# Gram matmuls whose moving side has 224 columns in place of 256

## The chip, the cores and the metric

The kernel runs on one core of a Trainium2 chip. Its metric is the device time of one execution in microseconds (us); lower is better. Before the change it took 532.54 us in the median of 3 runs (530.84 to 533.41).

## The reference, cut to what matters

A batch of 2048 samples, each with 27 feature vectors of 128 numbers. For each sample the dot products of every two features are formed (the gram matrix, 27 x 27), its 351 entries under the diagonal are put behind the sample's 128 dense numbers, and four layers with relu and one output row follow:

```python
dots = jnp.einsum('bfd,bgd->bfg', bottom_output, bottom_output)      # 2048 x 27 x 27
pairs = dots[:, _TRIL_I, _TRIL_J]                                    # 351 per sample
x = jnp.concatenate([bottom_mlp_output, pairs, pad], axis=1)         # 480
for w, b in ((w0, b0), (w1, b1), (w2, b2), (w3, b3)):                # 1024, 1024, 512, 256
    x = jax.nn.relu(x @ w.T + b)
return x @ w_out.T + b_out
```

Everything is float32.

## The kernel before, in words

Each engine has a program of its own, written out by hand; semaphores order them. The batch goes in 8 chunks of 256 samples. While TensorE multiplies the layers of chunk c, the grams of chunk c+1 are made between these products, and the first few of c+2. `chunk_steps` writes the order: after every 18 products of a chunk (6 in the first chunk) one list of `unit_steps` is put in, for one unit of 16 samples. A chunk has 16 units. A unit is four groups of four samples; a group is one matmul.

To reach nearly float32 results with the faster float32r matmuls, each operand is split into a high part that float32r holds exactly and the low remainder. A layer's product is then three matmuls (`products`, L726): high weights by high data, high weights by low data, low weights by high data, each with 128 x 128 weights and 256 columns moving.

A unit goes through these steps:

- SyncE loads its rows (L458). VectorE turns them, 32 x 32 at a time (L921), into `raw`, with the 128 numbers on the partitions and 32 columns for each sample, 27 of them features and 5 more.
- ScalarE writes the high part into `xt` (L805), VectorE the low part (L926), 27 columns of each sample's 32. `xt` holds for each group first 128 high columns, then 128 low ones. The 5 columns left of each sample are zero from a memset.
- TensorE multiplies (`gram`, L688): the 128 high columns are the weights, and the 256 columns, high and low, move. That gives high by high and high by low for all four samples against each other; only each sample against itself is of use. Two groups fill one PSUM bank of 512 numbers, and a unit has two banks. A gram waits until ScalarE has read the unit two before (`parts_done`).
- ScalarE reads the used blocks out of PSUM (`gram_parts`, L817), one instruction for each of the four samples' places: 27 partitions by 2 x 4 x 27 numbers, by the view `gram_found`.
- GpSimd adds high by low to high by high (L564), VectorE turns the high by low part (L945), GpSimd adds that too into `grams` (L571).

When a chunk's 16 units are done, SyncE writes `grams` to HBM (L405, `blocks<-grams`), reads them back in another order into `pairs` (L410), and then loads rows for the chunk after. The layers' results go from PSUM through ScalarE (`drain`, L833), then VectorE makes the high part (L952) and GpSimd the low (L579); TensorE's next layer waits for these.

The grams of chunk 0, before any layer, are made in another way: TensorE transposes (L647) and plain float32 matmuls with 128 x 128 weights and 108 columns (`gram_early`, L671). The weights are transposed by L642.

Of the kernel before, what the change touches and what calls it, by code (L numbers as in the profile page):

```python
# [11 lines left out]
BATCH, FEATS, DIM = 2048, 27, 128  # L12
PAIRS = FEATS * (FEATS - 1) // 2
LAYERS = [(DIM + PAIRS + 1, 1024), (1024, 1024), (1024, 512), (512, 256)]
P = 128
# [5 lines left out]
GROUP = 4  # L21
RUN = CHUNK // GROUP
GROUP_ROWS = GROUP * FEATS
QUAD = 32
# [27 lines left out]
ACC_RING, TURN_RING, GRAM_RING = 2, 2, 2  # L52
GRAM_BANKS = 2

XT_RING, XT_LAG = 4, 2
# [5 lines left out]
GATHER_AFTER, FIRST_UNIT, LATE_HOOK = 6, 11, 38  # L61
AHEAD, AHEAD_HOOK = 5, 49
FULL_ROWS = 112
EARLY_SLOTS = 8
RAW_RING = 2
EARLY_XT = 2 * XT_RING
# [157 lines left out]
def dlrm_program(nc, x, x_mlp, w0, b0, w1, b1, w2, b2, w3, b3, w_out, b_out, y):  # L224
    weights = [w0, w1, w2, w3]
    biases = [b0, b1, b2, b3]
    with ExitStack() as ctx:
        def sb(name, shape, dt=F32):
            return ctx.enter_context(nc.sbuf_tensor(name, shape, dt))
# [4 lines left out]
        def shared(*specs):  # L234

            with ExitStack() as inner:
                return [inner.enter_context(nc.sbuf_tensor(n, s, F32)) for n, s in specs]
# [13 lines left out]

        early_rows, = shared(("early_rows", [P, EARLY_SLOTS, UNIT_GROUPS, DIM]))
        h_b = sb("h_b", [P, 8, 2, CHUNK], F32R)
# [5 lines left out]
        xt = sb("xt", [P, XT_RING, UNIT_GROUPS, 2, GROUP * QUAD], F32R)  # L259
# [13 lines left out]
        gram_ps = ctx.enter_context(nc.psum_tensor("gram_ps", [P, GRAM_RING * GRAM_BANKS, 512], F32))  # L273
# [48 lines left out]
        step_n, step_u, step_c = FEATS * DIM, UNIT_GROUPS * GROUP * FEATS * DIM, CHUNK * FEATS * DIM  # L322
        full_dims = [[DIM, FULL_ROWS], [GROUP * step_n, UNIT_GROUPS], [1, DIM]]
        x_full = bass.AP(x.tensor, 0, [[step_c, CHUNKS - 1], [step_u, UNITS]] + full_dims)
# [68 lines left out]
        def quad_of(s):  # L393

            return slice(QUAD * s, QUAD * s + FEATS)

        def gram_found(u, s):

            b = u % GRAM_RING * GRAM_BANKS
            return gram_ps[quad_of(s), b:b + GRAM_BANKS, :].rearrange("p a (b h n) -> p h (a b) n", h=2, n=P)[  # L400
                :, :, :, QUAD * s:QUAD * s + FEATS]

        def spill_quad(engine, s):

# [7 lines left out]
        def early_rows_of(u):  # L412

            if u < EARLY_SLOTS:
                return early_rows[:, u]
            u -= EARLY_SLOTS
            return rows[:, u] if u < ROWS_RING else early_rows[:, u - ROWS_RING]
# [17 lines left out]
        def _(sp):  # L435
            def load_early(u):
                if u >= EARLY_SLOTS + ROWS_RING:

                    sp.wait_ge(turned, u - EARLY_SLOTS - ROWS_RING + 1)
                sp.dma_start(early_rows_of(u)[0:FULL_ROWS], x_full[0, u]).then_inc(early_loaded[u], 16)  # L440

            def load_rows(d, u):
                if isinstance(d, int) and d == 1 and u < ROWS_RING:

                    sp.wait_ge(turned, EARLY_SLOTS + u + 1)
                else:
# [152 lines left out]
        def _(pe):  # L599
# [75 lines left out]
            def gram(d, u):  # L675

                pe.wait_ge(xt_done, d * UNITS + u + 1)
                if isinstance(d, int) and d == 1 and u < GRAM_RING:
                    if u == 0:

                        pe.wait_ge(w_done, LATE_WEIGHTS)
                        pe.wait_ge(xt_zeroed, 2)
                else:

                    pe.wait_ge(parts_done, (d - 1) * UNITS + u + 1 - GRAM_RING)
                for j in range(UNIT_GROUPS):
                    at = j % 2 * 2 * P
                    last = nc.tensor.matmul(gram_ps[:, u % GRAM_RING * GRAM_BANKS + j // 2, at:at + 2 * P], xt[:, u % XT_RING, j, 0],  # L688
                                            xt[:, u % XT_RING, j].rearrange("p h n -> p (h n)"), start=True, stop=True)
                last.then_inc(gram_done, 1)  # L690

            def turn_mlp(d):
# [49 lines left out]
            def chunk(c):  # L742
                for step in steps_of(c):
                    if step[0] == "mm":
                        products(c, *step[1:])
                    elif step[0] == "gram":
                        gram(c + step[1], step[2])
                    elif step[0] == "weights":
                        turn_weights(step[1])
                    elif step[0] == "out" and not (isinstance(c, int) and c == 0):  # L750
                        out_row(c - 1)
                    elif step[0] == "mlp":
                        turn_mlp(c + 1)
# [20 lines left out]
        def _(act):  # L774
# [32 lines left out]
            def gram_parts(d, u):  # L807

                act.wait_ge(gram_done, d * UNITS + u + 1)
                if isinstance(d, int) and d == 1 and u < 2:  # L810

                    act.wait_ge(parts_zeroed, 1)
                else:

                    act.wait_ge(grams_done, d * UNITS + u - 1)
                for s in range(GROUP):
                    last = nc.scalar.activation(parts[quad_of(s), u % 2, :, :, 0:FEATS], gram_found(u, s), ACT.Copy)  # L817
                last.then_inc(parts_done, 1)
# [232 lines left out]
```

## Time and profile before

| | |
|---|---|
| median of 3 runs | 532.54 us |
| the profiled execution | 532.41 us |
| its span, first to last instruction | 530.6 us |
| TensorE matmuls busy | 501.3 us (94%) |
| VectorE, ScalarE, GpSimd busy | 289.1, 333.7, 260.6 us |
| gram matmuls, L688 | 448, 72.9 us of busy time |

The busy time of matmuls counts from the start of one to its modelled end, and these overlap: a matmul of 283 ns is followed by the next start 120 ns later. What a matmul costs in a dense stretch is therefore read as the distance of starts, not as its duration. The timeline merges neighbours; the distance is got from the starts of two rows and the count between them.

### The profile page before, as it was taken

Reading aid. Unit: us, or ns where it says so; the run is one execution under the profiler, and the core shown is the slowest. Engines: PE = TensorE matmul, PEld = TensorE weight load, DVE = VectorE, ACT = ScalarE, POOL = GpSimd, SP = SyncE. Lnnn points to the kernel's source line nnn. Section 1 sums busy time; section 2 is a strip of 40 time slices with the busy share of each in tenths; the row PEclk is TensorE's granted clock in tenths of the full one; section 3 lists DMA queues with packets and bytes.
Section 4 is the critical chain, followed back from the end, with each engine's and each line's share of the span. In section 5 each row is a group of like instructions: output and inputs, shape, how many; then the busy total and the mean of one; then the engine's idle time right before and its main releaser. Section 6 shows DMA issues by size and latency. Waiting matters only on the chain.

```text
span 530.6 us, 13442 instructions
## 1 busy us (share of the span) xinstructions
PE 501.3 (94%) x4073; PEld 491.5 (93%) x4073; DVE 289.1 (54%) x646; ACT 333.7 (63%) x844; POOL 260.6 (49%) x467
## 2 busy tenths in 40 slices
PE   6968987799999999999999999999999999999996
PEld 6858987699999899999999999999999999999996
DVE  3764877466753576446762676356753676232101
ACT  4644799747974588737883698657873698433112
POOL 2800356424865267634864287625764387524221
PEclk9996999999999999999999999999999999999999
DMA  8997677644563566356663656266653662210000
GB/s 246 264 312 156 196 119 114 114 77 81 89 109 75 94 105 104 55 109 113 102 96 67 116 96 106 44 125 109 99 79 79 117 103 43 49 47 1 1 1 0
DMA packets 281054, 53.23 MB, mean 100 GB/s; under 512 B 265126, under 2 KB 279230, under 8 KB 281022
## 3 DMA queue, kind: packets, MB, share of 16 engines
q1 hardware_dynamic: 279090, 52.22, 51.9%
q10 hardware_dynamic: 1932, 0.61, 0.5%
q8 instruction: 17, 0.28, 0.2%
q14 instruction: 15, 0.12, 0.1%
HBM read 45.71 MB, written 7.09 MB: 99 GB/s over the span
## 4 chain that ended last, share of the span: by engine, by line
PE 66%; DMA 11%; SPq 7%; ACT 5%; POOL 4%; issue 4%; DVE 3%; POOLq 0%; DVEq 0%; ACTq 0%
PE acc L726 52%; PE gram_ps L688 8%; DMA blocks<-grams 5%; ACT parts L817 3%; SPq L410 3%; DMA early_rows<-in_r_bottom_output_dram 2%; SPq L405 2%; PE gram_ps L642 2%; DMA rows<-in_r_bottom_output_dram 2%; PE gram_ps L671 2%; POOL grams L571 1%; SPq L458 1%; POOL h_a L579 1%; POOL parts L564 1%; DMA pairs<-blocks 1%
## 5 line engine op out<-in xcount | busy, mean ns | idle before, releaser
L726 PE MATMUL acc<-h_a,w_hi 128*128 128x256 f32 x1152 | 214.4, 285 | 3.9 <-POOL h_a L579 2.6
L726 PEld LDWEIGHTS acc<-h_a,w_hi 128*128 128x128 f32 x1152 | 179.1, 192 | 6.6 <-POOL h_a L579 4.3
L817 ACT ACTIVATE parts<-gram_ps 27x216 f32<-27x216 f32 x448 | 152.9, 341 | 25.7 <-PE gram_ps L688 18.5
L833 ACT ACTIVATE h_full<-acc,small_t 128x256 f32<-128x256 f32 x172 | 81.5, 474 | 132.2 <-PE acc L726 128.7
L726 PE MATMUL acc<-h_a,w_lo 128*128 128x256 f32 x576 | 162.8, 283 | 0.0
L579 POOL TENSOR_TENSOR h_a<-h_full,h_a 128x256 fp32r<-128x256 f32 x96 | 72.2, 752 | 139.6 <-DVE h_a L952 139.6
L726 PEld LDWEIGHTS acc<-h_a,w_lo 128*128 128x128 f32 x576 | 110.3, 192 | 0.0
L726 PE MATMUL acc<-h_b,w_hi 128*128 128x256 f32 x512 | 93.9, 284 | 0.0
L726 PE MATMUL acc<-x,w_hi 128*128 128x256 f32 x480 | 90.7, 288 | 0.0
L579 POOL TENSOR_TENSOR h_b<-h_full,h_b 128x256 fp32r<-128x256 f32 x64 | 47.4, 740 | 83.1 <-DVE h_b L952 83.1
L564 POOL TENSOR_TENSOR parts<-parts 128x128 f32<-128x128 f32 x112 | 82.4, 736 | 6.1 <-ACT parts L817 5.5
L926 DVE TENSOR_TENSOR xt<-raw,xt 128x432 fp32r<-128x432 f32 x112 | 82.0, 732 | 4.2 <-ACT xt L805 4.2
L921 DVE STREAM_TRANSPOSE raw<-rows 128x512 f32<-128x512 f32 x112 | 78.4, 700 | 6.2 <-DMA rows<-in_r_bottom_output_dram 6.0
L726 PEld LDWEIGHTS acc<-h_b,w_hi 128*128 128x128 f32 x512 | 79.7, 192 | 0.0
L688 PE MATMUL gram_ps<-xt 128*128 128x256 f32 x448 | 72.9, 285 | 6.3 <-ACT parts L817 5.9
L726 PEld LDWEIGHTS acc<-x,w_hi 128*128 128x128 f32 x480 | 75.5, 194 | 1.4 <-issue 0.8
L952 DVE CAST h_a<-h_full 128x256 fp32r<-128x256 f32 x96 | 32.2, 336 | 80.1 <-ACT h_full L833 80.1
L726 PE MATMUL acc<-h_b,w_lo 128*128 128x256 f32 x256 | 72.4, 283 | 0.0
L688 PEld LDWEIGHTS gram_ps<-xt 128*128 128x128 f32 x448 | 61.6, 192 | 8.8 <-DVE xt L926 4.4
L952 DVE CAST h_b<-h_full 128x256 fp32r<-128x256 f32 x64 | 18.8, 294 | 93.2 <-ACT h_full L833 93.2
L726 PE MATMUL acc<-x,w_lo 128*128 128x256 f32 x240 | 68.3, 285 | 0.0
L805 ACT ACTIVATE xt<-raw 128x432 fp32r<-128x432 f32 x112 | 62.5, 558 | 1.8 <-DVE raw L921 1.4
(59 smaller groups left out, 439.5 us busy)
## 6 DMA issues: line engine op xcount, KB each, us to landing
rows<-in_r_bottom_output_dram SPq DMA_DIRECT2D x444, 64.0 KB, 2.1
blocks<-grams SPq DMA_DIRECT2D x30, 216.0 KB, 3.9
w_raw<-in_L_rec_w_dram SPq DMA_DIRECT2D x6, 1024.0 KB, 7.9
early_rows<-in_r_bottom_output_dram SPq DMA_DIRECT2D x12, 224.0 KB, 5.7
stage_pairs<-in_L_rec_w_dram SPq DMA_DIRECT2D x1, 1408.0 KB, 9.2
w_raw<-in_L_rec_w_dram SPq DMA_DIRECT2D x2, 512.0 KB, 8.5
mlp_rows<-r_bottom_mlp_output_dram SPq DMA_DIRECT2D x8, 128.0 KB, 2.2
pairs<-blocks SPq DMA_DIRECT2D x8, 126.0 KB
```

The costliest lines, as they stand in the source:

```text
L405: engine.dma_start(blocks[:, :, s * RUN:(s + 1) * RUN], grams[QUAD * s:QUAD * (s + 1)]).then_inc(spilled, 16)
L410: engine.dma_start(pairs[q % P:q % P + nf * nk, q // P], src).then_inc(gathered[q // P], 16)
L564: nc.gpsimd.tensor_tensor(hh, hh, hl, ALU.add).then_inc(sum_done, 1)
L579: nc.gpsimd.tensor_tensor(h[:, m, 1, :], h_full[:, slot % 2, :], h[:, m, 0, :].bitcast(F32), ALU.subtract).then_inc(split_done, 1)
L688: last = nc.tensor.matmul(gram_ps[:, u % GRAM_RING * GRAM_BANKS + j // 2, at:at + 2 * P], xt[:, u % XT_RING, j, 0], xt[:, u % XT_RING, j]. ...
L726: last = nc.tensor.matmul(acc_slot(c, slot), weight(wp, layer, m, k), in_tile(layer, k, xp), start=(k == 0 and n == 0), stop=(k == K_TILES ...
L805: nc.scalar.activation(xt_part(u, 0), raw_cols(u), ACT.Copy).then_inc(xt_hi_done, 1)
L817: last = nc.scalar.activation(parts[quad_of(s), u % 2, :, :, 0:FEATS], gram_found(u, s), ACT.Copy)
L833: nc.scalar.activation(h_full[:, slot % 2, :], acc_slot(c, slot), ACT.Relu, bias=small_t[:, slot:slot + 1]).then_inc(drained, 1)
L921: nc.vector.transpose(raw[:, u % RAW_RING].rearrange("p j n -> p (j n)"), rows[:, r].rearrange("p j n -> p (j n)")).then_inc(raw_turned, 1)
L926: nc.vector.tensor_tensor(xt_part(u, 1), raw_cols(u), xt_part(u, 0).bitcast(F32), ALU.subtract).then_inc(xt_done, 1)
L952: nc.vector.tensor_copy(h[:, m, 0, :], h_full[:, slot % 2, :]).then_inc(high_done, 1)
```

## The change

The gram matmul's moving side reads, of each sample's 32 columns, the first 28 (27 features and one zero column) in place of all 32: 2 x 4 x 28 = 224 columns. Its outputs lie packed 28 apart, 224 numbers from the same starts in the bank. ScalarE's view of PSUM follows. The weights' side, the number of instructions, their order and all waits stay; on TensorE the 112 rows of four gram matmuls stand in the same places with 128x224 for 128x256.

```diff
+EVEN = FEATS + 1
...
         def gram_found(u, s):
 
             b = u % GRAM_RING * GRAM_BANKS
-            return gram_ps[quad_of(s), b:b + GRAM_BANKS, :].rearrange("p a (b h n) -> p h (a b) n", h=2, n=P)[
-                :, :, :, QUAD * s:QUAD * s + FEATS]
+            found = gram_ps[quad_of(s), b:b + GRAM_BANKS, :].rearrange("p a (b n) -> p (a b) n", n=2 * P)
+            return found[:, :, 0:2 * GROUP * EVEN].rearrange("p j (h n) -> p h j n", h=2)[
+                :, :, :, EVEN * s:EVEN * s + FEATS]
...
                 for j in range(UNIT_GROUPS):
                     at = j % 2 * 2 * P
-                    last = nc.tensor.matmul(gram_ps[:, u % GRAM_RING * GRAM_BANKS + j // 2, at:at + 2 * P], xt[:, u % XT_RING, j, 0],
-                                            xt[:, u % XT_RING, j].rearrange("p h n -> p (h n)"), start=True, stop=True)
+                    found = gram_ps[:, u % GRAM_RING * GRAM_BANKS + j // 2, at:at + 2 * GROUP * EVEN]
+                    both = xt[:, u % XT_RING, j].rearrange("p h (s f) -> p (h s) f", f=QUAD)[:, :, 0:EVEN]
+                    last = nc.tensor.matmul(found, xt[:, u % XT_RING, j, 0], both, start=True, stop=True)
                 last.then_inc(gram_done, 1)
```

## Rows read from the trace of the kernel before

**Rows 1.** The page, part 1: busy time of each engine.

```profile
PE 501.3 (94%) x4073; PEld 491.5 (93%) x4073; DVE 289.1 (54%) x646; ACT 333.7 (63%) x844; POOL 260.6 (49%) x467
```

**Rows 2.** Stretches: length, busy us and count of each engine, clock, DMA, GB/s.

```profile
80.00:120.00 40.00, 33.57 (x269) 31.97 (x269) 24.57 (x51) 28.49 (x71) 16.88 (x29) 1.00 0.58 101
120.00:180.00 60.00, 59.87 (x497) 59.42 (x496) 34.97 (x77) 42.21 (x111) 34.60 (x54) 1.00 0.50 86
41.00:44.00 3.00, 2.96 (x15) 2.96 (x15) 0.43 (x1) 0.56 (x2) 0.00 (x0) 0.50 0.72 135
```

**Rows 3.** Timeline of TensorE in a dense stretch: start, length, instruction, count.

```profile
128.77 0.64 PE L688 MATMUL gram_ps<-xt 128*128 128x256 f32 x4
129.25 0.40 PE L726 MATMUL acc<-x,w_hi 128*128 128x256 f32 x2
129.49 0.28 PE L726 MATMUL acc<-x,w_lo 128*128 128x256 f32 x1
```

**Rows 4.** Line L688: duration ns min/median/max, first and last start, form.

```profile
L688 PE MATMUL gram_ps<-xt x448: 278/283/357, 65.5 to 456.9; 128*128 128x256 f32 x150
```

**Rows 5.** Tile `parts` from 120 us on, same columns: readouts and GpSimd's sums.

```profile
L817 ACT ACTIVATE parts<-gram_ps x382: 320/343/348, 120.0 to 458.3; 27x216 f32<-27x216 f32 x191
L564 POOL TENSOR_TENSOR parts<-parts x96: 457/826/911, 122.3 to 458.7; 128x128 f32<-128x128 f32 x96
```

**Rows 6.** Who TensorE waited for, 65 to 120 us: total, times, longest.

```profile
PE gram_ps L688 <- ACT parts L817: 5.9, 9, 0.8
```

**Rows 7.** The same view, 120 to 500 us.

```profile
PE acc L726 <- POOL h_a L579: 2.6, 5, 1.0
PE acc L726 <- ACT h_full L833: 1.0, 5, 0.2
```

**Rows 8.** Timeline of ScalarE, 83 to 89 us.

```profile
83.82 1.41 ACT L817 ACTIVATE parts<-gram_ps 27x216 f32<-27x216 f32 x4 [0.19 <-POOL grams L571]
85.26 0.57 ACT L805 ACTIVATE xt<-raw 128x432 fp32r<-128x432 f32 x1
85.85 1.41 ACT L817 ACTIVATE parts<-gram_ps 27x216 f32<-27x216 f32 x4
87.28 0.47 ACT L833 ACTIVATE h_full<-acc,small_t 128x256 f32<-128x256 f32 x1
```

**Rows 9.** The chain that ended last, 221 to 244 us: start, length, what.

```profile
222.75 0.49 PE gram_ps L688 x4
225.29 0.59 POOL grams L571
228.23 4.43 DMA blocks<-grams
237.60 1.94 DMA rows<-in_r_bottom_output_dram
241.96 0.87 POOL h_a L579
```

**Rows 10.** Timeline, the two output-row matmuls with one column of weights.

```profile
308.17 0.39 PE L739 MATMUL turned_ps<-h_a,ones 128*1 128x256 f32 x2
308.40 0.40 PE L726 MATMUL acc<-x,w_hi 128*128 128x256 f32 x2
```

**Rows 11.** Line L671, the plain float32 grams of chunk 0.

```profile
L671 PE MATMUL gram_ps<-xt_full x128: 275/275/421, 7.0 to 28.7; 128*128 128x108 f32 x128
```

**Rows 12.** Timeline of TensorE there.

```profile
26.15 2.84 PE L671 MATMUL gram_ps<-xt_full 128*128 128x108 f32 x24
```

**Rows 13.** Timeline of weight loads: float32 grams, then float32r grams.

```profile
26.17 2.54 PEld L671 LDWEIGHTS gram_ps<-xt_full 128*128 128x128 f32 x22
...
304.93 0.55 PEld L688 LDWEIGHTS gram_ps<-xt 128*128 128x128 f32 x4
```

**Rows 14.** Timeline of TensorE at half clock: layer products, 256 columns.

```profile
42.59 0.63 PE L726 MATMUL turned_ps<-x,w_hi 128*128 128x256 f32 x2
43.02 0.41 PE L726 MATMUL turned_ps<-x,w_lo 128*128 128x256 f32 x1
```

## The prediction

> **What bounds the kernel now.** I read the busy times first. TensorE's matmuls are busy for 94% of the span, no other engine for more than 63% [rows 1]. Then the stretches, to see whether that holds everywhere: from 120 us on TensorE is busy for 59.87 of 60 us, while from 80 to 120 us it is busy for 33.57 of 40 [rows 2]. So there are two regimes. In the long one each matmul that becomes shorter makes the kernel shorter. In the short one, where the grams of chunk 1 lie between the products of chunk 0, something else sets the pace: TensorE waits nine times for ScalarE's readout of grams, 5.9 us in all [rows 6], and ScalarE's instructions stand there nearly end to end (83.82 + 1.41 = 85.23, the next at 85.26; 85.26 + 0.57 = 85.83, the next at 85.85) [rows 8].
>
> Third, the pace of matmuls in the dense stretch. Four gram matmuls start at 128.77 and the next product at 129.25: 0.48 / 4 = 120 ns each. The two products behind them take 0.24 / 2 = 120 ns each [rows 3]. The duration of one, 283 ns [rows 4], is no cost, since they overlap. The gram matmuls cost 448 x 120 ns = 54 us, and the change touches only these.
>
> Last, the chain at a chunk's end. After the last gram of a chunk (222.75) it runs through GpSimd's sum, the writing of the grams to HBM, a load of rows, and GpSimd's split of the last layer's input at 241.96, for which TensorE waits [rows 9]. From 120 us on that wait adds up to 2.6 us over five boundaries [rows 7]. The matmuls of two units lie beside this chain, not in it.
>
> **The change, part by part.** Nothing is added, removed or moved; 448 matmuls (112 units of four) [rows 4] stream 224 columns in place of 256. Three further things change in form.
>
> 1. The streaming. At the full level of the clock, 2.4 GHz (granted clock 1.00 [rows 2]), 256 columns at one a cycle would be 106.7 ns and 224 would be 93.3 ns, 13.3 ns less. That one column a cycle fits is seen at the other level: where the granted clock was 0.50, three products took (43.02 - 42.59) / 2 = 215 ns each [rows 14], which is 256 columns at 1.2 GHz (213). At the full level 120 - 107 = 13 ns are on top. The question is whether 120 falls by all of the 13.3.
>
> 2. The weight load. Each gram matmul brings a new 128 x 128 block of float32 weights, and this stays. No row shows float32r with fewer than 256 columns, so I bound it. The nearest rows are the float32 grams of chunk 0: 24 instructions with 128 x 128 weights and only 108 columns take 2.84 us, or (2.84 - 0.28) / 23 = 111 to 112 ns each [rows 12]. Their weight loads keep the same distance, (2.54 - 0.19) / 21 = 112 ns [rows 13], where I took 0.19 us for one load from (0.55 - 0.19) / 3 = 120 ns in the second row there. With so few columns it is most likely the load that sets 112 ns. The other side: with one column of weights and 256 moving, a matmul takes (308.40 - 308.17) / 2 = 115 ns [rows 10]. So streaming alone is 115, loading alone about 112, and both together 120. With 224 columns streaming alone would be 115 - 13 = 102, under the load. The ends are therefore: 120 (no gain, whatever sets 120 does not see the columns) and 120 - 13.3 = 106.7 (all of it gained). I take 112, the row with the same weights and fewer columns: 8 ns less for each matmul.
>
> The Trainium skill ("TensorE: Matmul & The Clock Gate", section "LDWEIGHTS (loading the stationary operand)") says that a load's time goes with the number of weight columns alone, P/1.2 ns, which is 107 ns for 128: by it the floor would be 107 and the gain at most 13 ns. The measured 112 decides.
>
> 3. The moving side is read in 8 runs of 28 numbers with gaps of 4, before in one run. The float32 grams read 4 runs of 27 with gaps of 5, and take 112 ns all the same [rows 12]. So I put this at nothing; if each run cost a cycle, 8 x 0.42 = 3 ns would be hidden under the load as well.
>
> 4. ScalarE reads the same 216 numbers from 27 partitions, 28 apart in place of 32. Nothing in the rows has such a step alone; the ends are 0 and a tenth of its 343 ns [rows 5] up or down, and I take 0. In the dense stretch it is hidden (42.21 of 60 us busy [rows 2]).
>
> The sum. Dense stretch: the units of chunks 2 to 7 are 96 (the GpSimd sums from 122 us on are x96 [rows 5]), so 384 matmuls x 8 ns = 3.1 us. Of these the two units beside each of five end-of-chunk chains, 40 matmuls x 8 = 0.3 us, gain nothing if that chain [rows 9] holds its length: the wait for GpSimd grows by as much. That leaves 2.8 us. Chunk 1's 16 units, 64 matmuls x 8 = 0.5 us, lie where ScalarE sets the pace [rows 6, 8]; TensorE comes 32 ns earlier to the same wait. I take 0.1 of the 0.5. The sum is 2.9 us, with 2.8 and 3.6 as ends for 8 ns.
>
> What is late next: nothing new in the dense stretch. ScalarE, at 42.21 of 60 us, gets each gram 32 ns earlier, and SyncE's writing of a chunk's grams starts earlier with it.
>
> The profiled execution took 532.41 us, so the sum gives 529.5; the median of the runs shown is 532.54, which gives 529.6. That is 0.55% faster. This measurement can tell about 0.5%, 2.7 us, from no change, so the forecast sits on that edge.
>
> **The rivals.**
>
> *Nothing is gained.* The 120 ns are set by the pair of a 128-column load and its matmul, whatever streams. For it: load and matmul both keep exactly 120 [rows 3, 13], and alone they are 112 and 115, so 120 is neither of them. Against it: at 108 columns the same load goes at 112 [rows 12]. Time: 532.5.
>
> *All of the streaming is gained.* The load is hidden and 120 falls to 107 ns. 384 x 13.3 = 5.1, plus part of chunk 1's 0.85 and less 0.5 at the boundaries: about 5 us, up to 6.0 (448 x 13.3). Time: 527.5, down to 526.5. Against it: no matmul with 128 x 128 weights is seen under 111 ns [rows 12]. The skill's rule for the distance of matmuls (the same page, "Back-to-back issue gap", N/2.4 + 2.5 ns) stands on this side, with 109 ns for 256 columns and 96 for 224; the trace's 120 for 256 already disagrees with it.
>
> *The matmul falls out of its fast form, and the kernel is slower.* Every float32r matmul here has exactly 256 columns; the trace has none with fewer. If float32r with fewer columns went as plain float32 does, each gram matmul would cost what L671's does: that line has 64 matmuls in the code (16 units of four) and 128 in the trace, two for each, 2 x 112 = 224 ns for 108 columns [rows 11, 12]. The lower end is 224 ns for our 224 columns too, (224 - 120) x 448 = 47 us, and by columns it is 224 x 224 / 108 = 465 ns, 155 us. Time: 579 to 687. It decides from 126 ns for a gram matmul, since 6 x 448 = 2.7 us. For it: only that no row excludes it, and that float32 already shows such a doubling in this trace. Against it: the loads of float32 and float32r go alike (112 and 120), which looks like one machine with a floor, not two modes.
>
> *The gapped reading costs.* Place: the same matmuls, 120 to about 128 ns, up to 3.6 us slower, 536. The float32 grams' 112 with gaps speaks against it.
>
> **How the numbers follow.** Forecast (a gram matmul at 111 to 114 ns, 1.8 to 3.6 us less): 0.50. Nothing gained: 0.24. All gained: 0.12. Out of the fast form: 0.10. Gapped reading: 0.04. The forecast lies on the edge of 0.5%, so a little over half of it counts as faster: 0.28 of 0.50, the rest as no change. Faster: 0.28 + 0.12 + 0.01 from noise = 0.41. No change: 0.22 + 0.23 = 0.45. Slower: 0.10 + 0.04 = 0.14. The range reaches from the end of "all gained" (526.5, less half a us of spread) to "nothing gained" with the spread that the three runs show (533.41) and a part of the gapped reading: 526.0 to 534.5. It leaves the third rival out. The forecast's own range is 528.3 to 531.5.
>
> **What would show it.** In the timeline of a dense stretch, four gram matmuls from the first start to the next product's start: 0.45 us by the forecast (0.48 before), 0.48 if nothing is gained, 0.43 if all is, 0.9 or more with twice the instructions if they fall out of the fast form. The distance of their weight loads should equal it. TensorE's wait for GpSimd at the five boundaries should rise by some 0.05 us each, and its waits for ScalarE in chunk 1's stretch should grow by about 0.3 us in all. The readouts of ScalarE should stay at 343 ns, the products of the layers at 120. The prediction is wrong if a gram matmul's distance is under 110 or over 115 ns, or if it is 112 and the time does not follow.

## The result and the profile after

The changed kernel took 530.85 us in the median of 22 runs (528.97 to 534.53), the kernel before 534.40 beside it (22 runs, 530.16 to 537.26). The ratio is 0.9956, interval 0.9938 to 0.9975: about 2.4 us, a small gain that is clear of noise. (The two medians alone lie 3.55 us apart, a ratio of 0.9934. I go by the ratio and its interval, which two profiles agree with.) The forecast was 529.6 from 532.54, a ratio of 0.9945. So the time and the direction of that number hold. The chances beside it did not: they had "no change" as the likeliest (0.45 to 0.41), because they treated 0.5% as the least that can be told. The interval here is 0.2% wide on either side and leaves "no change" out.

The profiled execution took 531.61 us. The page's rows that answer to [rows 1, 4]:

```profile
span 529.8 us, 13442 instructions
...
PE 497.5 (94%) x4073; PEld 486.9 (92%) x4073; DVE 289.7 (55%) x646; ACT 333.4 (63%) x844; POOL 260.6 (49%) x467
...
L692 PE MATMUL gram_ps<-xt 128*128 128x224 f32 x448 | 68.7, 276 | 6.8 <-ACT parts L820 6.3
```

There are still 448 instructions, not twice as many, so nothing fell out of the fast form. The span is only 0.8 us shorter, though. The reason stands ahead of anything the change touches. These rows give, for L688 and L692 from chunk 2 on, the first and last start, before and after:

```profile
L688 PE MATMUL gram_ps<-xt x384: 279/283/283, 118.6 to 456.9; 128*128 128x256 f32 x192
```

```profile
L692 PE MATMUL gram_ps<-xt x384: 270/274/278, 120.3 to 456.1; 128*128 128x224 f32 x192
```

Chunk 2's first gram comes 1.7 us later in the profile after, and the first gram of all (67.2 against 65.5) is as much later. Over the profiles of this study that first gram started anywhere from 62.9 to 69.0 us, while weights and rows are loaded. So profiles are compared here by what follows chunk 2's first gram: 530.6 - 118.6 = 412.0 us before, 529.8 - 120.3 = 409.5 after. I call this the rest. It is 2.5 us shorter, which agrees with the ratio; a second profile of the changed kernel gives 409.6.

The dense stretch, TensorE's timeline, answering to [rows 3]:

```profile
212.99 0.60 PE L692 MATMUL gram_ps<-xt 128*128 128x224 f32 x4
213.43 0.41 PE L729 MATMUL acc<-h_a,w_hi 128*128 128x256 f32 x2
213.67 0.28 PE L729 MATMUL acc<-h_a,w_lo 128*128 128x256 f32 x1
```

Four gram matmuls now take 213.43 - 212.99 = 0.44 us, 110 ns each, where they took 0.48. From one unit to the next it is 2600 ns in place of 2640: 10 ns for each matmul, 3.8 us over 96 units. Only 2.5 of it arrived. TensorE's waits from 120 us on, answering to [rows 7]:

```profile
PE acc L729 <- POOL h_a L581: 3.0, 5, 1.1
PE acc L729 <- ACT h_full L836: 1.0, 5, 0.2
```

At the five ends of chunks it waits 0.4 us more than before. The remaining 1.0 us does not appear in this view; the one of the weight loads (PEld) shows where it is. The first fence is of before, the second of after, both for PEld from 120 us on:

```profile
PEld acc L726 <- POOL h_a L579: 4.3, 7, 1.2
```

```profile
PEld acc L729 <- POOL h_a L581: 5.7, 12, 1.3
```

The wait for GpSimd's low part has 12 cases in place of 7: one more in five of the six chunks (in the sixth it is shorter and is not listed). One of them in the timeline, first the same place before, then after:

```profile
202.92 0.51 PE L726 MATMUL acc<-h_a,w_hi 128*128 128x256 f32 x2
203.26 0.28 PE L726 MATMUL acc<-h_a,w_lo 128*128 128x256 f32 x1
```

```profile
203.60 0.19 PEld L729 LDWEIGHTS acc<-h_a,w_lo 128*128 128x128 f32 x1
203.72 0.28 PE L729 MATMUL acc<-h_a,w_lo 128*128 128x256 f32 x1
...
204.01 0.30 PEld L729 LDWEIGHTS acc<-h_a,w_hi 128*128 128x128 f32 x2 [0.22 <-POOL h_a L581]
204.02 0.50 PE L729 MATMUL acc<-h_a,w_hi 128*128 128x256 f32 x2
204.36 0.28 PE L729 MATMUL acc<-h_a,w_lo 128*128 128x256 f32 x1
```

This is layer 1 waiting for the last slot of layer 0 (a slot is one block of 128 outputs; its products end in one drain). After, there are 300 ns between two matmul starts, where 120 is the pace, and another 0.10 us inside the pair that follows (0.34 us to the third start in place of 0.24). Before, only that 0.10 was there. So the unit around it takes 2.86 to 2.88 us in five chunks, 0.26 to 0.28 over its neighbours, where it took 2.74, 0.10 over. In the sixth chunk it is 2.79 against 2.63. Each chunk gives back 0.15 to 0.19 us there, 1.0 us in six: 3.8 - 1.0 - 0.4 = 2.4.

What stands ahead of that slot's drain is seen on ScalarE, in the changed kernel:

```profile
200.91 1.41 ACT L820 ACTIVATE parts<-gram_ps 27x216 f32<-27x216 f32 x4 [0.34 <-POOL grams L573]
202.34 0.48 ACT L836 ACTIVATE h_full<-acc,small_t 128x256 f32<-128x256 f32 x1
```

Four readouts stand right ahead of the drain, and they had themselves waited 0.34 us for GpSimd's sums of an earlier unit (the same four waited 0.28 before). Behind the drain come VectorE's high part and GpSimd's low part, which ends at 203.96; the load starts at 204.01. Nor has ScalarE much room there. In the trace of before, over 13 us in which its drains are those of a layer 0, it is busy for 12.04 us (the fourth engine of the row):

```profile
189.00:202.00 13.00, 13.00 (x111) 12.93 (x110) 9.64 (x22) 12.04 (x32) 10.57 (x17) 1.00 0.59 96
```

### The profile page after: what moved, and what is told of

Read it like the earlier page. It is cut to its first block, busy times and chain, and to the rows that moved or that the text cites. A ratio compares the mean times of both kernels' runs of the same rounds, so it can differ in the third digit from the quotient of the medians.

```text
span 529.8 us, 13442 instructions
## 1 busy us (share of the span) xinstructions
PE 497.5 (94%) x4073; PEld 486.9 (92%) x4073; DVE 289.7 (55%) x646; ACT 333.4 (63%) x844; POOL 260.6 (49%) x467
## 4 chain that ended last, share of the span: by engine, by line
PE 58%; DMA 11%; POOL 9%; issue 7%; SPq 7%; ACT 4%; DVE 3%; POOLq 0%; DVEq 0%; ACTq 0%
PE acc L729 46%; PE gram_ps L692 6%; DMA blocks<-grams 5%; ACT parts L820 3%; POOL parts L566 3%; SPq L412 3%; DMA early_rows<-in_r_bottom_output_dram 2%; POOL grams L573 2%; SPq L407 2%; POOL h_a L581 2%; PE gram_ps L644 2%; DMA rows<-in_r_bottom_output_dram 2%; PE gram_ps L673 2%; POOL h_b L581 1%; DMA pairs<-blocks 1%
## 5 line engine op out<-in xcount | busy, mean ns | idle before, releaser
L692 PE MATMUL gram_ps<-xt 128*128 128x224 f32 x448 | 68.7, 276 | 6.8 <-ACT parts L820 6.3
L692 PEld LDWEIGHTS gram_ps<-xt 128*128 128x128 f32 x448 | 59.7, 192 | 9.3 <-DVE xt L929 4.6
```

The costliest lines, as they stand in the source:

```text
L692: last = nc.tensor.matmul(found, xt[:, u % XT_RING, j, 0], both, start=True, stop=True)
```

## The experiments

All start from the changed kernel unless said. First, the size of the gain: what holds a gram matmul at 110 ns. (c240 and w64 ran once each, so their units stand for them and no ratio.)

**c128: 128 columns.**

```diff
-found = gram_ps[..., at:at + 2 * GROUP * EVEN];  both = xt[...][:, :, 0:EVEN]
+found = gram_ps[..., at:at + 2 * GROUP * 16];    both = xt[...][:, :, 0:16]
```

> The changed kernel with a moving side of 16 columns per sample, 128 in place of 224 (the columns of features 16 to 27 are left out of the grams; readouts unchanged). In a dense stretch a unit (18 products and four gram matmuls) took 2640 ns with 256 columns and 2600 with 224. Theory A, the weight load of 128 columns sets a floor near 110 ns: a unit stays at 2600 (within 10), the gram matmuls at 110 to 112 ns, the time at a ratio of 0.994 to 0.998 of before, as the change itself. Theory B, the columns set the pace down to their own number: 128 columns are 53 ns, a gram matmul goes at about 67 ns, a unit takes 2430, and the time falls by up to 15 us (ratio 0.97). Theory C, fewer than 256 columns in float32r lose speed per column somewhere below: a gram matmul over 120 ns.

```profile
213.26 0.56 PE L692 MATMUL gram_ps<-xt 128*128 128x128 f32 x4
213.66 0.46 PE L729 MATMUL acc<-h_a,w_hi 128*128 128x256 f32 x2
```

The first gram matmul starts 120 ns after the product ahead of it. From there the distances of starts are 63, 111, 112 and 111 ns up to the first product behind the group, and 173 ns from that one to the next. The short 63 and the long 173 make up for each other, and the unit is what counts: 2607 ns, or (2607 - 18 x 120) / 4 = 112 ns for each gram matmul. Ratio 0.9972 (0.9938 to 1.0006). Taking away 96 more columns buys nothing: theory A. The weight loads say the same. From the second load of the group to the second behind it, their starts are 111 to 112 ns apart in this run and in the changed kernel alike, though one streams 128 columns and the other 224. The run had one thing more. Chunk 1 took 54.6 us in place of 53.1, with the clock granted at half in parts of it:

```profile
80.00:86.00 6.00, 5.16 (x32) 4.99 (x31) 4.16 (x11) 5.62 (x16) 3.70 (x7) 0.72 0.78 122
98.00:104.00 6.00, 6.00 (x40) 6.00 (x40) 2.57 (x5) 2.86 (x5) 1.14 (x2) 0.72 0.66 141
```

The granted clock (third from the end) is 0.72, a mean of the two levels. It stood at 1.00 in both stretches of the changed kernel's second profile.

**c240: 240 columns.** The same edit with 30 for 16. (Its readout keeps the steps of 28 while the outputs lie 30 apart, so it picks other columns than the grams'; the expectation overlooked that.)

> 30 columns per sample, 240 moving, nothing left out. Theory A (a pace of the longer of load, about 111, and streaming with its 13 ns, 240/2.4 + 13 = 113): a unit of 2605 to 2615 ns, four gram matmuls in 0.45 us. Theory B' (columns count one for one, 10 ns for the 32 taken away): half of the gain, 2620. If float32r had a step at 256 columns and none other, 240 would be as 224: 2600.

```profile
214.21 0.63 PE L692 MATMUL gram_ps<-xt 128*128 128x240 f32 x4
214.67 0.40 PE L729 MATMUL acc<-h_a,w_hi 128*128 128x256 f32 x2
```

A unit takes 2625 ns: 15 saved for 16 columns of each matmul, 25 more for the next 16. There is no step at 256, and no pure floor either: theory A's 2605 to 2615 was missed on the high side, and 2625 lies nearer to theory B' with 2620. Near the crossing, load and streaming together cost more than the longer of them alone: 116 ns here, where the load takes 112 and streaming 115 - 7 = 108 (an estimate from [rows 10]). Why they do is open.

**run224: the 224 columns in one run.**

```diff
-both = xt[:, u % XT_RING, j].rearrange("p h (s f) -> p (h s) f", f=QUAD)[:, :, 0:EVEN]
+both = xt[:, u % XT_RING, j].rearrange("p h n -> p (h n)")[:, 0:2 * GROUP * EVEN]
```

> 224 columns read as one run in place of 8 runs of 28 (other columns than the readout expects; the last sample's low part is left out). Theory that gaps cost nothing: a unit of 2600 ns and a ratio to before within 0.002 of the change's 0.9956. Theory that the 8 gaps cost some of the expected 13 ns: a unit of 2590 or less, 3 ns less for each gram matmul, 1 us less in all.

A unit takes 2600 to 2601 ns, the rest is 408.7. Ratio 0.9928 (0.9898 to 0.9958), which is 0.0028 from the change's and not within the 0.002 expected, but overlaps its interval. Gaps cost nothing that the units show. The profile's rest is 0.8 us under the change's for another reason: the long wait at the end of chunk 2 was 0.7 us shorter.

**w64: 64 weight columns.**

```diff
-nc.tensor.matmul(found, xt[:, u % XT_RING, j, 0], both, ...)
+nc.tensor.matmul(found[0:64], xt[:, u % XT_RING, j, 0, 0:64], both, ...)
```

> The changed kernel with 64 of the 128 weight columns (the grams of the samples at places 2 and 3 are left out; readouts unchanged), 224 moving. Theory A, the load sets the floor: half the load frees the streaming, a gram matmul falls to 98 to 103 ns, a unit to about 2560 ns. If it stays at 110 ns and 2600, the floor is not the number of weight columns. If switching the shape of the array costs, the first and last of the four grow.

```profile
213.92 0.58 PE L692 MATMUL gram_ps<-xt 128*64 128x224 f32 x4
214.34 0.42 PE L729 MATMUL acc<-h_a,w_hi 128*128 128x256 f32 x2
```

105 ns each over the group, a unit of 2587 ns, which makes (2587 - 18 x 120) / 4 = 107. The direction is A's: with half the weight columns and the same 224 moving the matmuls are faster, with the same weights and 128 moving they are not. So the load is what held them at 110. The size fell short of the expected 98 to 103. What holds them at 105 to 107 is open: no run had 64 weight columns with 256 moving, and the run also writes half as many outputs.

Second, where the missing 1.4 us went.

**a_lite and b_lite: one readout less for ScalarE**, in the changed kernel and in the one before.

```diff
-for s in range(GROUP):
+for s in range(GROUP - 1):
     last = nc.scalar.activation(parts[quad_of(s), ...], gram_found(u, s), ACT.Copy)
```

> The changed kernel with three of the four PSUM readouts of each unit on ScalarE (the fourth sample's grams are left out): 343 ns less for ScalarE in every unit. Theory P (part of what each gram saves is given back because ScalarE and what follows it set the pace in chunk 1 and in each layer 0): the new wait of TensorE at the start of layer 1 (297 ns between two starts near 204 us in the changed kernel) is gone (under 200 ns), chunk 1's stretch from its first gram to chunk 2's first falls from 53.1 us by more than 1.5 us, and against its twin with 256 columns the time from chunk 2's first gram to the last is shorter by 3.6 us or more (95 x 40 ns = 3.8), where with four readouts it was 2.45 us. Theory Q (the give-back is a transfer's or an order's, not ScalarE's): the difference to the twin stays at 2.2 to 2.7 us.

> The twin: the kernel before, 256 columns, with three of the four readouts (the fourth sample's grams left out). Units of 2640 ns. By theory P its own gain over the kernel before lies in chunk 1 (over 1.5 us) and little in the dense chunks (its wait at layer 1 was only about 0.1 us a chunk), and the change is worth 3.6 us or more from here (ratio a_lite to b_lite about 0.993). By theory Q the change is worth the same 2.4 us as with four readouts (0.9955).

Ratios to before: 0.9771 (0.9722 to 0.9821) and 0.9870 (0.9817 to 0.9923); between the two that is 0.990, where 0.993 was expected by theory P. Chunk 1, first gram to first gram, fell from 53.1 to 49.4 and 49.9 us. The grams from chunk 2 on, a_lite and then b_lite:

```profile
L692 PE MATMUL gram_ps<-xt x384: 270/274/278, 114.0 to 445.9; 128*128 128x224 f32 x192
```

```profile
L688 PE MATMUL gram_ps<-xt x384: 279/283/283, 114.6 to 450.0; 128*128 128x256 f32 x192
```

From the first to the last it is 331.9 against 335.4: the change is worth 3.5 us here, 2.45 with four readouts. The wait at layer 1 is gone in both. Theory P had said 3.6 or more; the missing 0.3 is at the ends of chunks, where a_lite still waits 2.3 us and b_lite 1.9. The size of P's figure was missed by a little, its place was right: P holds for layer 0, and the ends of chunks are a second, separate place.

**s21 and s21e: other distances between units.** The order tables get a list of distances in place of the constant 18. It is shown here in short, for the 14 units that complete a chunk's grams; two units of the chunk after follow.

```diff
-HOOK = 18 for all units of a chunk
+s21:  [21]*4 + [18]*6 + [15]*4
+s21e: [21]*4 + [15]*10
```

> The changed kernel, complete, with the units of the dense chunks spread otherwise: after 21 products each in layer 0 (four units), 18 in the next six, 15 in the last four, the last at the same place as before. Theory P: in layer 0, where each unit falls beside more drains, ScalarE gets more room, the wait at layer 1 (297 ns) falls under 150 ns, and each chunk ends 0.1 to 0.2 us earlier: 0.6 to 1.0 us less than the change alone, ratio to before about 0.994. If ScalarE now falls behind in the tight last four (15 products and a gram: 2.24 us, against 0.57 + 4 x 0.34 + 0.3 = 2.26 us of ScalarE), the gram waits there and nothing is won or 0.5 us lost.

> The same with 15 products between the ten units after layer 0: the last gram of a chunk comes 18 products (2.2 us) earlier. If the chain from the last gram through the writes and loads of SyncE ends in TensorE's wait at a chunk's end (0.7 to 0.8 us, 1.3 once), that wait falls by 0.2 us or more at each of five boundaries, and the time is 1 us or more under s21. If that wait is the layers' own (drain, high part, low part of the last input: 0.48 + 0.3 + 0.74 us), it stays at 0.65 and s21e is as s21, or slower by what the tight units cost ScalarE.

s21 is slower, 1.0048 (1.0009 to 1.0087), s21e as before, 1.0000 (0.9964 to 1.0035). My expectation for s21 failed. (ScalarE's sum in it comes to 2.23 us, not 2.26.) The wait at layer 1 went, but two others came in layer 0, of 0.48 and 0.36 us between two starts, and the waits for GpSimd at the ends of chunks grew from 3.0 to 4.5 us. ScalarE's timeline in s21:

```profile
191.01 1.41 ACT L825 ACTIVATE parts<-gram_ps 27x216 f32<-27x216 f32 x4 [0.51 <-PE gram_ps L697]
192.44 0.92 ACT L841 ACTIVATE h_full<-acc,small_t 128x256 f32<-128x256 f32 x2
```

TensorE's next product started at 192.97, after a wait for that `h_full`. The four readouts, 1.41 us, now stand ahead of two drains, and with two accumulator banks TensorE cannot run that far ahead. So what counts is not how much room ScalarE has on average but what stands ahead of a drain. s21e has the same two waits in layer 0. The part of s21e's expectation on the ends of chunks held: with the last gram 2.2 us earlier each of the five waits there was 0.66 us between starts, where the change has 0.70 to 1.33.

**e15 and m24: a chunk's end and layer 0's end by themselves.** **b_m24** is m24's order on the kernel before; **again** is the changed kernel once more, run beside them.

```diff
+e15: [18]*8 + [15]*6                    # last gram 18 products earlier
+m24: [18]*4 + [24] + [15]*9             # the fifth unit behind layer 0's last product, last gram 21 products earlier
```

> The changed kernel, complete, layer 0 as it was (a unit after each 18 products for the first eight), then 15 for the last six: a chunk's last gram comes 18 products (2.2 us) earlier. Expected from the spread with 15 after layer 0, whose waits at a chunk's end were 0.66 us each: TensorE's wait for GpSimd at the five boundaries falls from 0.70 to 1.33 us to 0.66 us each, 1.0 to 1.2 us in all, the wait at layer 1 (297 ns) stays, no new wait in layer 0; from chunk 2's first gram to the first gram of the last chunk made, chunk periods of 58.0 in place of 58.16. If the wait at a chunk's end is the layers' own alone, nothing changes.

> As e15, and the fifth unit is put behind layer 0's last product (24 products after the fourth), so that its four readouts stand behind the drain of layer 0's last slot on ScalarE, not ahead of it; then 15 between units. If ScalarE's readouts ahead of that drain make the wait at layer 1, that wait (297 ns) falls to 120 to 130 ns, 6 x 0.17 = 1.0 us less than e15: chunk periods of 57.8 to 57.9, ratio to before about 0.992. If the wait stays, it is GpSimd's or VectorE's queue.

> The kernel before (256 columns) in m24's order. If the change is worth its 40 ns in every unit once nobody else sets the pace, m24's chunk periods lie 16 x 40 = 640 ns under these (in the present order the distance is 0.36 to 0.48 us), so 58.45 to 58.55 here.

> The changed kernel itself, beside the three others: units of 2600 ns, chunk periods of 58.15 with one of 58.7, a ratio to before of 0.994 to 0.998.

| kernel | ratio to before (interval) | rest, us | chunk to chunk, us |
|---|---|---|---|
| before | 1 | 412.0 | 58.5 to 58.6, once 59.2 |
| again | 0.9942 (0.9914 to 0.9971) | 409.6 | 58.0 to 58.2, once 58.7 |
| e15 | 0.9945 (0.9916 to 0.9974) | 408.7 | 58.0 to 58.05 |
| m24 | 0.9889 (0.9850 to 0.9928) | 407.1 | 57.7 to 57.8 |
| b_m24 | 0.9996 (0.9965 to 1.0028) | 410.8 | 58.4 |

The last column is the distance of the first grams of two neighbouring chunks. The waits from 125 us on in m24:

```profile
PE acc L734 <- POOL h_a L586: 1.9, 5, 0.4
PE acc L734 <- ACT h_full L841: 1.0, 5, 0.2
```

and ScalarE's order where layer 0 ends, the drain of the last slot now ahead of the readouts:

```profile
204.33 0.47 ACT L841 ACTIVATE h_full<-acc,small_t 128x256 f32<-128x256 f32 x1 [0.60 <-PE acc L734]
204.70 0.56 ACT L813 ACTIVATE xt<-raw 128x432 fp32r<-128x432 f32 x1
205.16 1.39 ACT L825 ACTIVATE parts<-gram_ps 27x216 f32<-27x216 f32 x4
```

e15 removes the extra at the ends of chunks (3.0 to 1.9 us) and keeps the wait at layer 1 (291 ns). It shortens the rest by 0.9 us against again, which is too little for the ratio to show. m24 removes both, and its last gram comes another 3 products earlier, which takes nothing more off the waits for GpSimd (1.9 us in both). From b_m24 to m24 a chunk is shorter by 58.43 - 57.78 = 0.65 us, which is 16 x 40 = 640 ns: with nobody else setting the pace, the change is worth all of its 10 ns per matmul. In the rest it is 410.8 - 407.1 = 3.7 us. The ratios, 0.9889 and 0.9996, are 5.7 us apart and their intervals do not overlap; why they show more than the rest is open. The order by itself is worth little to the kernel before: 1.2 us in the rest, nothing clear in the ratio. (Its chunks of 58.4 us came a little under the 58.45 to 58.55 expected.) m24 is the fastest complete kernel here, though its profiled execution has a long span (532.0): its first gram came at 69.0 us, and chunk 1 took 55.9 us with the granted clock at a mean of 0.62 from 101 to 110 us:

```profile
101.00:110.00 9.00, 6.91 (x36) 6.91 (x37) 3.00 (x6) 4.24 (x10) 2.52 (x6) 0.62 0.58 116
```

m24's order of chunk 1 is the changed kernel's. Whether such a stretch is likelier in one kernel than another is open; the profiles show it in c128, w64, s21, e15 and m24, and not in the others, the two of the change among them.

## Why the prediction came out as it did

Two steps failed. One was the time of the dense stretch: "nothing new in the dense stretch" put a wait at nothing that took back 1.0 us. The other was the measurement: "about 0.5%, 2.7 us" as the least that can be told rests on no row, and it turned a forecast of 2.9 us less into "no change" as the likeliest outcome.

- *Regimes.* Right. Chunk 1's length did not move: 53.1 us in both profiles (0.1 us was expected), and its waits for ScalarE's readouts grew by 0.4 us (0.3 was expected). With one readout less chunk 1 fell by over 3 us, so ScalarE sets the pace there.
- *The weight load as a floor.* Right as a mechanism, shown by c128 and w64. The size was 8 ns in the sum and 10 measured (110, not 112): 3.8 us, not 3.1. The loads themselves do go at 112. By its own sign the prediction would have been wrong under 110 ns, and 110 is just at that edge. One rival used the formula N/2.4 + 2.5 ns for the distance of matmuls. The Trainium skill ("TensorE: Matmul & The Clock Gate", section "Back-to-back issue gap") gives this formula for a matmul by itself and says that in a stream of loads and matmuls both set the distance. So it was no evidence for that rival. The trace of c128 agrees: 112 ns for 128 columns, where the formula alone gives 56.
- *Gapped reading and readout.* Right: nothing. The readouts stayed at 343 ns.
- *Ends of chunks.* The chain beside two units was named and priced at 0.3 us; it took 0.4. e15 and m24 show that it can be had back by an earlier last gram.
- *"What is late next: nothing new in the dense stretch."* This is the step that failed. I took ScalarE's 42 of 60 busy us as room. It is a mean over all layers; where its drains are layer 0's, the same trace has 12.04 of 13. In layer 0 a drain comes after every 12 products, and a unit's four readouts stand ahead of the drain of its last slot; behind it come VectorE's and GpSimd's parts, and layer 1. That chain already bound once a chunk by 0.1 us, and the trace of before had it (a unit of 2.74 us among units of 2.64). It took back 1.0 us. a_lite and m24, each without this wait, show it.
- *The sum.* 3.8 - 1.0 - 0.4 = 2.4 against 2.9. The errors were +0.7 (the gain of one matmul), -1.0 (layer 1) and -0.1 each at the ends of chunks and in chunk 1. That the forecast came so near is in part luck, since they partly cover each other.
- *The chances.* This step failed too. The mechanism that I gave 0.50 is the one that came. But a forecast of 0.55% was split by the bound of 0.5%: 0.22 of the 0.50 went to "no change", beside the 0.23 of "nothing gained". What 22 runs of each kernel showed in place of the bound is an interval of 0.2% to either side, so the measured 0.44%, though under 0.5%, is a change. Without the split, faster would have had 0.63.

## What to carry to other kernels

Before a matmul is made narrower, look for a row with the same weights and fewer columns: it shows where the load takes over, here at about 110 ns for 128 float32 columns. The first 32 columns under 256 were worth 10 ns, the 96 under those nothing. Then ask at each layer's first wait what stands ahead of the awaited drain on its engine; a unit that is longer than its neighbours by a tenth of a microsecond marks a chain that will take the gain. Moving the readouts behind that drain and the last gram earlier was worth as much again as the change itself, 2.5 us of the rest, and less (1.2 us) on the kernel with 256 columns.

## What the runs showed of the hardware

- In a stream of float32r matmuls that each bring 128 x 128 weights, at a granted clock of 1.00, one goes at 120 ns with 256 columns, about 116 with 240, 110 with 224 and 112 with 128 (units of 2640, 2625, 2600, 2607 ns in before, c240, after, c128). None of the three narrower widths is slower than 256.
- With 64 weight columns and 224 moving it goes at 105 to 107 ns (w64: by the group, and by the unit of 2587 ns).
- A moving side in 8 runs of 28 numbers costs no more than the same 224 in one run (units of 2600 ns in after and run224).
- Starts of matmuls are not the pace one by one: with 128 columns the second of four came 63 ns after the first, and the second product behind them 173 ns after the first product. Only the distance over a whole unit can be added up.
